# Attention between two expert layers on one core: weighted sums turned by VectorE in 32x32 blocks, quotients on GpSimd, a new order of jobs

## The chip, the cores and the metric

One Trainium2 chip, one of its cores. The metric is the device time of one execution in microseconds; the numbers before are the median of three executions.

## The reference, cut to what matters

```
x = L0_attn_x                                   # (32, 256, 128): 32 sequences of 256 tokens
x = x + 0.5 * ffn(layernorm(x))                 # 8 routed experts (top 2) + a shared one, swiglu
x = x + attn(layernorm(x))
x = x + 0.5 * ffn(layernorm(x))

def attn(x):                                    # 16 heads of 8 features
    Q, K, V = x @ W_Q.T, x @ W_K.T, x @ W_V.T
    s = where(causal, Q @ K.T / sqrt(8), -inf)
    return (softmax(s) @ V) @ W_O.T
```

The change is in `attn`; the two expert layers are computed as before.

## The kernel before, in words

The kernel runs three stages one behind the other: expert layer, attention (`attention_phase`, line 800), expert layer. x stays in SBUF throughout. Tokens are worked on in 16 chunks of 512, so a chunk of the attention is two sequences (b = 0 and 1).

**Units.** Each sequence has four units (j = 0 to 3) of four heads, so a chunk is eight units, called u0 to u7 here (u = 4b + j). A head has 32 rows in the packed tables `q_pack` and `k_pack`: three places of 8 rows with high and low halves of q and k in float16, so that one product gives the float32 accuracy, and at row 24 a place for the row's maximum. A unit uses the 32 rows of its own j in four groups.

The scores are computed twice. First as queries x keys (`scores`, line 999), only to find each row's maximum: three thirds, each a PSUM bank of 128x512 with the causal mask laid in by a product (L983) and the heads' products on top (L993); VectorE reduces each (`maxima`, L1167). This runs five units ahead. The two score banks are used in turn, so a third waits for the reduction two thirds back (line 977). The jobs m turn the negated maxima into a row of `q_pack`. Then, in the unit itself, the scores come as keys x queries with the maximum already subtracted (`scores_t`, L1025), again three thirds, each with a bank of its own; ScalarE takes the exponents into `probs` (L1241) and GpSimd sets what lies beyond the diagonal to zero (two `affine_select`, L1282). `weigh` (L1065) multiplies by V one unit later. V's table `v_ones` has a column of ones for each head, so the sum of the weights comes out with the weighted sum; the four groups write to four 32-row strips of `o_bank`, and ScalarE copies them to `o_t` (L1247).

**Jobs.** Everything else is a job, run between the units in the order of the list `PLACES` (line 761), and each job writes one of two PSUM banks in turn: a job cannot begin before the one two places ahead has been taken. x: four transposes of the normalised rows. q, k: three products of 128x512 each. Q and K (four each in a chunk, named by sequence and half): the rows of q or k are put into their places of the packed tables by two products with a 0/1 table (L926). v: twelve products. m: see above. o (four in a chunk): four transposes of `o_t` (L940), so that VectorE can take reciprocals (L1144) and multiply (L1146). y (two): two transposes of the quotients back (L949), split by ScalarE (L1231) and VectorE (L1152). z (two): the product with W_O, and VectorE adds it to x (L1155).

**Order.** Each engine runs its own list by hand. TensorE in a unit (`turn`, line 1070): thirds 0 and 1 of the unit's keys x queries product and of the scores five units ahead, interleaved so that neighbours use different rows of the array (`both`, line 1038), then third 2 of the first kind; then the first place's jobs; `weigh` of the unit before; third 2 of the scores ahead; and the jobs of the other two places. VectorE: two reductions, jobs, the third reduction, jobs; the layer norm of the chunk two ahead in u5, its scaling (L110) in u6. ScalarE: three exponents, jobs, the copy of `o_bank`. GpSimd: two masks a unit, and in u5 the inverse root of the norm (L94, an `ALU.pow` over 128x4).

To split q, ScalarE and VectorE write "stacks": a tile with the high halves of 64 rows and the low halves of the same rows, so each takes two instructions of 64 rows (L1215, L1129). Half of the Q jobs are taken by VectorE (L1134), half by ScalarE (L1219).

Of the kernel before, what the change touches and what calls it, by code (L numbers as in the profile page):

```python
# [5 lines left out]
ALU = mybir.AluOpType  # L6
# [19 lines left out]
MAX_ROW = 3 * HEAD  # L26
SCALE = float(HEAD) ** -0.5
# [34 lines left out]
LN_STEPS = 2 * TILES  # L62

# [162 lines left out]
def ffn_phase(nc, x, consts, w, norms, phase, x_dram, out, gates_dram, prepare=None):  # L226

    with ExitStack() as ctx:  # L228
# [267 lines left out]
        def _(pe):  # L496
# [91 lines left out]
            def keep_busy(n):  # L588

                pe.wait_ge(x_added, CHUNKS - 1)  # L590
                for _ in range(n):
                    nc.tensor.matmul(y_bank[CHUNKS % 2][:, :], w["w1_hi"][:, 0, :], xt_hi[turned(CHUNKS - 1)][:, :],
                                     start=True, stop=True)
# [137 lines left out]
SELECT_PARTS = 2 * 2 * ROWS // HEAD  # L731
# [3 lines left out]
def select_heads(nc, consts, done, part):  # L735

    ident = consts["ident"][:, :].rearrange("p (g j d) -> p g j d", g=GROUPS, j=UNITS)
    half = GROUPS // 2
    name, low_place = (("sel_q", 2), ("sel_k", 1))[part // (SELECT_PARTS // 2)]
    place, first = part // 2 % (ROWS // HEAD), part % 2 * half  # L740
    table = consts[name][:, :, :].rearrange("p g (j r) -> p g j r", r=ROWS)
    dst = table[:, first:first + half, :, place * HEAD:(place + 1) * HEAD]
    if place == MAX_ROW // HEAD:
        nc.vector.tensor_scalar(dst, ident[:, first:first + half, :, :], 0.0, None, ALU.mult).then_inc(done, 1)
    else:
        src = half - first if place == low_place else first
        nc.vector.tensor_copy(dst, ident[:, src:src + half, :, :]).then_inc(done, 1)


def select_max_row(nc, consts, done):  # L750
# [45 lines left out]
WARM = {"Q00": 7, "K00": 3, "Q01": 1, "first": 4}  # L796
# [3 lines left out]
def attention_phase(nc, x, consts, w, norms):  # L800

    with ExitStack() as ctx:
# [6 lines left out]
        def sem(name):  # L809
# [11 lines left out]
        stack = {m: [sb(f"{m}_stack{half}", [P, CHUNK], F16) for half in range(2)] for m in "qk"}  # L821
        half_rows = (slice(0, P // 2), slice(P // 2, P))
# [19 lines left out]
        xhi_done, qkhi_done, yhi_done, inv_done = (sem(n) for n in ("xhi_done", "qkhi_done", "yhi_done", "inv_done"))  # L842
        mask_begun = sem("mask_begun")
        scored, max_done = sem("scored"), sem("max_done")
        st_done, exp_done, masked, pv_done, o_done = (
            sem(n) for n in ("st_done", "exp_done", "masked", "pv_done", "o_done"))
# [35 lines left out]
        def _(pe):  # L882
# [14 lines left out]
            def keep_busy(n):  # L897

                for _ in range(n):
                    nc.tensor.matmul(o_bank[:, :], w_hi[:, 0, :], xt_hi[:, :], start=True, stop=True)  # L900

            def job(c, slot, name):
# [15 lines left out]
                elif kind in "QK":  # L918
# [15 lines left out]
                elif kind == "o":  # L934

                    b, t = int(name[1]), int(name[2])
                    pe.wait_ge(o_done, c * 2 * UNITS + (b + 1) * UNITS)
                    dst, done = begin(c, name)
                    for j in range(UNITS):
                        last = nc.tensor.transpose(dst[:, j * P:(j + 1) * P], o_t[b][:, j, t * P:(t + 1) * P],  # L940
                                                   ident[:, :])
                elif kind == "y":
                    b = int(name[1])

                    wait_taken(pe, c, f"o{b}0")
                    wait_taken(pe, c, f"o{b}1")
                    dst, done = begin(c, name)
                    for t in range(2):
                        last = nc.tensor.transpose(dst[:, t * P:(t + 1) * P], y[:, t, :], ident[:, :])  # L949
                elif kind == "z":  # L950

                    wait_taken(pe, c, "y" + name[1])
# [16 lines left out]
            def begin_scores(c, b, j, i):  # L969

                if j == 0 and i == 0:

                    wait_taken(pe, c, f"Q{b}1")
                    wait_taken(pe, c, f"K{b}1")
# [401 lines left out]
```

## Time and profile before

| | us |
|---|---|
| median of three runs (lowest, highest) | 1211.31 (1208.91, 1214.98) |
| the profiled execution, its own time | 1214.04 |
| its span | 1212.3 |
| first expert layer | 0 to 330.4 |
| attention | 330.4 to 899.8 |
| second expert layer | 899.8 to 1212.3 |

Over the whole span TensorE is busy for 93%, VectorE 83%, ScalarE 65% and GpSimd 47%. "Busy" counts an instruction from its start to its modelled end, and neighbouring products overlap, so for TensorE the start-to-start distances say more than the busy share. Granted clock 1.00 is the higher of two levels (2.4 GHz), 0.5 the lower. PEld is the loading of weights, which runs ahead of the products.

### The profile page before, as it was taken

The numbers are of one execution on the slowest core, as the hardware profiler recorded it, in microseconds if no ns is written. First come the engines' busy times: TensorE is split into PE (matmuls) and PEld (weight loads), VectorE is DVE, ScalarE is ACT, GpSimd is POOL, SyncE is SP. The second block draws the span as 40 slices with busy tenths as digits, with TensorE's granted clock in tenths as the row PEclk, the third lists the DMA queues.
The fourth block names the chain that finished last, engine by engine and source line by source line (L and its number), as shares of the span: only waits on it lengthen the run. The fifth ranks groups of instructions, "written<-read, shape, count | busy, mean of one in ns | idle before, by whom it ended". The sixth has DMA issues, their size and how long they took to land. (4 is left out here: it accounts for less than half of the span.)

```text
span 1212.3 us, 32050 instructions
## 1 busy us (share of the span) xinstructions
PE 1124.4 (93%) x11615; PEld 691.2 (57%) x11615; DVE 1002.0 (83%) x2583; ACT 789.4 (65%) x1545; POOL 567.7 (47%) x728
## 2 busy tenths in 40 slices
PE   3899999999989999999899999999978999999998
PEld 1566666666635555555555555555545666666665
DVE  4889999999657877888888788888758898998985
ACT  4676766767536665676676667676646667667664
POOL 2566666666603322333333223333325666666655
PEclk9899999999969998999999899999988999999999
DMA  4442443432200000000000000000004434435443
GB/s 125 153 159 90 149 144 101 136 129 85 70 1 2 2 2 1 2 2 2 2 2 2 2 2 2 2 1 2 2 2 141 145 101 151 126 114 158 117 122 97
DMA packets 59866, 80.13 MB, mean 66 GB/s; under 512 B 5568, under 2 KB 26944, under 8 KB 59712
## 3 DMA queue, kind: packets, MB, share of 16 engines
q1 hardware_dynamic: 59712, 78.08, 20.8%
q8 instruction: 96, 1.57, 0.5%
q14 instruction: 58, 0.48, 0.1%
HBM read 73.34 MB, written 4.72 MB: 64 GB/s over the span
## 5 line engine op out<-in xcount | busy, mean ns | idle before, releaser
L709 POOL TENSOR_TENSOR h_lo<-h,h_hi 128x512 f16<-128x512 f32 x288 | 333.5, 1158 | 233.9 <-ACT h_hi L656 231.8
L1167 DVE TENSOR_REDUCE neg_max_at<-score_at 128x2 f16<-128x512 f32 (+1 forms) x384 | 254.1, 691 | 80.1 <-PE score_at L993 74.9
L1282 POOL TENSOR_SCALAR_AFFINE_SELECT probs_at<-probs_at 128x512 f32<-128x512 f32 x256 | 156.3, 634 | 343.6 <-ACT probs_at L1241 343.6
L1241 ACT ACTIVATE probs_at<-prob_at 128x512 f32<-128x512 f32 x384 | 201.7, 599 | 77.3 <-PE prob_at L1025 75.2
L648 ACT ACTIVATE a<-a 128x512 f32<-128x512 f32 x256 | 149.0, 582 | 132.6 <-PE a L549 127.6
L435 DVE TENSOR_TENSOR prod<-a,gate_wide 128x512 f32<-128x512 f32 x256 | 176.0, 687 | 40.9 <-ACT a L648 40.1
L565 PE MATMUL y_b<-w_hi,h_hi 128*128 128x128 f16 x1152 | 207.8, 219 | 1.3 <-POOL h_lo L709 1.3
L565 PE MATMUL y_b<-w_lo,h_hi 128*128 128x128 f16 x1152 | 207.8, 219 | 0.0
L565 PE MATMUL y_b<-w_hi,h_lo 128*128 128x128 f16 x1152 | 207.8, 219 | 0.0
L656 ACT ACTIVATE h_hi<-h 128x512 f16<-128x512 f32 x288 | 179.5, 623 | 16.1 <-DVE h L445 15.5
L445 DVE TENSOR_TENSOR h<-prod,b 128x512 f32<-128x512 f32 x256 | 174.3, 681 | 4.9
L983 PE MATMUL score_at<-causal,ident_b 128*128 128x256 bf16 (+1 forms) x384 | 110.5, 325 | 32.0 <-ACT q_pack_at L1219 15.2
L993 PE MATMUL score_at<-k_pack_at,q_pack_at 32*128 32x128 f16 (+1 forms) x1024 | 134.4, 251 | 0.0
L565 PEld LDWEIGHTS y_b<-w_hi,h_hi 128*128 128x128 f16 x1152 | 112.7, 98 | 28.5 <-issue 1.6
L565 PEld LDWEIGHTS y_b<-w_lo,h_hi 128*128 128x128 f16 x1152 | 112.7, 98 | 27.1
L1065 PE MATMUL o_at<-probs_at,v_ones_at 128*32 128x256 f32 (+1 forms) x2048 | 116.2, 347 | 1.7 <-POOL probs_at L1282 1.7
L565 PEld LDWEIGHTS y_b<-w_hi,h_lo 128*128 128x128 f16 x1152 | 112.7, 98 | 0.0
L549 PE MATMUL a<-xt_hi,w_hi 128*128 128x512 f16 x288 | 110.6, 384 | 0.4 <-DVE prod L435 0.4
L549 PE MATMUL a<-xt_hi,w_lo 128*128 128x512 f16 x288 | 110.6, 384 | 0.0
L549 PE MATMUL a<-xt_lo,w_hi 128*128 128x512 f16 x288 | 110.3, 383 | 0.0
L549 PE MATMUL b<-xt_hi,w_hi 128*128 128x512 f16 x288 | 110.2, 383 | 0.0
L549 PE MATMUL b<-xt_hi,w_lo 128*128 128x512 f16 x288 | 110.2, 383 | 0.0
(143 smaller groups left out, 1988.3 us busy)
## 6 DMA issues: line engine op xcount, KB each, us to landing
gate_wide<-gate_rows SPq DMA_DIRECT2D x256, 256.0 KB, 5.4
x<-in_L_attn_x_dram SPq DMA_DIRECT2D x16, 256.0 KB, 6.0
out_dram<-x SPq DMA_DIRECT2D x16, 256.0 KB, 6.9
raw_w<-in_L_ffn_w_dram SPq DMA_DIRECT2D x3, 512.0 KB, 5.3
gate_rows<-gate_rows SPq DMA_DIRECT2D x32, 16.0 KB, 1.4
raw_w<-in_L_ffn_sw_dram SPq DMA_DIRECT2D x3, 64.0 KB, 3.9
raw_attn<-in_L_attn_W_Q_dram SPq DMA_DIRECT2D x1, 64.0 KB, 4.8
raw_attn<-in_L_attn_W_K_dram SPq DMA_DIRECT2D x1, 64.0 KB, 3.0
```

The costliest lines, as they stand in the source:

```text
L435: nc.vector.tensor_tensor(prod[k][:, :], a_bank[k][:, :], gate_wide[c % 2][:, e - 1, :], ALU.mult).then_inc(prod_done, 1)
L445: nc.vector.tensor_tensor(h[e % 3][:, :], prod[k][:, :], b_bank[k][:, :], ALU.mult).then_inc(h_done, 1)
L549: last = nc.tensor.matmul(dst[k][:, :], ws[:, e, :], xs[s][:, :], start=(i == 0), stop=(i == 2))
L565: last = nc.tensor.matmul(y[:, tile], hs[k][:, tile], ws[:, e, :], start=(e == 0 and t == 0 and i == 0), stop=(e == STEPS - 1 and t == TIL ...
L648: nc.scalar.activation(dst[:, :], a_bank[k][:, :], ACT.Silu).then_inc(silu_done, 1)
L656: nc.scalar.activation(h_hi[k][:, :], h[k][:, :], ACT.Copy).then_inc(hhi_done, 1)
L709: nc.gpsimd.tensor_tensor(h_lo[k][:, :], h[k][:, :], h_hi[k][:, :], ALU.subtract).then_inc(hlo_done, 1)
L993: last = nc.tensor.matmul(view[:, h, :], q_pack[slot][rows, groups[h], q0:q0 + P], k_pack[slot][rows, groups[h], first:first + keys], star ...
L1065: last = nc.tensor.matmul(o_bank[g * ROWS:(g + 1) * ROWS, t * P:SEQ], v_ones[slot][:, 2 * b + t, GROUPS * g + j, :], src, start=(t == 0), ...
L1167: nc.vector.tensor_reduce(dst, src, AX.X, ALU.max, negate=True).then_inc(max_done, 1)
L1241: nc.scalar.activation(probs[j % 2][:, i, :], prob_bank[i][:, :], ACT.Exp, scale=SCALE).then_inc(exp_done, 1)
L1282: nc.gpsimd.affine_select(out=p, in_=p, compare_op=ALU.is_ge, fill=0.0, base=0, pattern=[[0, GROUPS], [1, P]], channel_multiplier=-1).then ...
```

## The change

Six edits, all in the attention stage but for a table set up in the first expert layer.

- **o and y.** The jobs o and y are gone, and ScalarE's copy of `o_bank` with them. Two heads now share a 32-row strip (`OUT_ROWS` = 16 rows each), and all four units of a sequence stay in the one bank. At the start of the next sequence VectorE turns the bank in 32x32 blocks (`divide`, step 0, 128x512 float32), GpSimd takes the quotients (`quotient`: `pow` with -1 over 128x32, then a product over 128x256), VectorE turns them back one unit later (step 1, 128x256), ScalarE takes the high half (`split_y`), GpSimd the low (`low_y`).
- **q and k** are split as whole 128x512 tiles: one instruction of each engine per tile. A Q or K job now has four products (high table with high half, low with low) where it had two. All Q jobs are ScalarE's.
- **Banks.** Three score banks, one for each third, so that a third waits for the reduction three back; two banks for the keys x queries product, thirds 0 and 2 in one, so third 0 waits for the exponents of the unit before, and third 2 for those of third 0.
- **Third 2** of the keys x queries product is moved behind `weigh` and interleaved with third 2 of the scores (`thirds`), and ScalarE's third exponent behind the first place's jobs.
- **Norm.** Statistics and roots in u1, with a shift computed by GpSimd; the scaling is ScalarE's, in u2 and u3, two tiles each.
- **Jobs** are laid out anew in `PLACES`, 18 where there were 24, q two chunks ahead. The products that only keep TensorE busy before the stage read weights in place of the normalised x.

```diff
+OUT_ROWS = ROWS // 2
...
-PLACES = (((), ("q",), ("k",)), (("o10",), ("o11",), ("Q00",)), (("K00",), ("Q01",), ("K01",)),
-          (("m10", "m11"), ("y1",), ()),
-          (("z1",), ("Q10",), ("K10",)), (("o00",), ("o01",), ("Q11",)), (("K11",), ("y0",), ("v",)),
-          (("m00", "m01"), ("x",), ("z0",)))
+PLACES = (((), ("k",), ("Q00",)), ((), (), ("K10", "K00")), (("K01", "Q01"), ("Q10",), ()),
+          (("m10", "m11"), ("v", "z1"), ()), ((), ("K11",), ()), ((), ("x", "Q11"), ()),
+          ((), (), ("z0",)), (("m00", "m01"), (), ("q",)))
 JOBS = [name for unit in PLACES for place in unit for name in place]
-SHIFT = {n: -2 if n == "x" else -1 if n in ("m00", "m01") or n[0] in "qkQKv" else 1 if n in ("o10", "o11", "y1", "z1")
-         else 0 for n in JOBS}
-BESIDE_FIRST = [JOBS.index(n) for n in ("m10", "o00", "y0", "m00", "m00")]
+SHIFT = {n: -2 if n in "xq" else -1 if n in ("m00", "m01") or n[0] in "qkQKv" else 1 if n == "z1" else 0 for n in JOBS}
+BESIDE_FIRST = [JOBS.index(n) for n in ("Q10", "m11", "z1", "Q11", "m00")]
...
-WARM = {"Q00": 7, "K00": 3, "Q01": 1, "first": 4}
+WARM = {"q-": 5, "Q00": 2, "K10": 2, "first": 3}
...
-        stack = {m: [sb(f"{m}_stack{half}", [P, CHUNK], F16) for half in range(2)] for m in "qk"}
-        half_rows = (slice(0, P // 2), slice(P // 2, P))
+        split = {m: [sb(f"{m}_{part}", [P, CHUNK], F16) for part in ("hi", "lo")] for m in "qk"}
...
-        o_t = [sb(f"o_t{s}", [P, UNITS, SEQ], F32) for s in range(2)]
-        inv = sb("inv", [P, 2, UNITS, GROUPS], F32)
-        y = sb("y", [P, 2, P], F32)
+        o_rows = sb("o_rows", [P, 2 * SEQ // ROWS, 2, OUT_ROWS], F32)
+        inv, minus = (sb(n, [P, 2 * SEQ // ROWS, 2], F32) for n in ("inv", "minus"))
+        y = sb("y", [P, 2, SEQ // ROWS, OUT_ROWS], F32)
+        yt = sb("yt", [P, SEQ], F32)
         yt_hi, yt_lo = sb("yt_hi", [P, SEQ], F16), sb("yt_lo", [P, SEQ], F16)
-        score_bank = [bank(f"score{s}") for s in range(2)]
-        prob_bank = [bank(f"prob{i}") for i in range(3)]
+        score_bank = [bank(f"score{i}") for i in range(3)]
+        prob_bank = [bank(f"prob{s}") for s in range(2)]
...
+        def v_places(slot):
+            return v_ones[slot][:, :, :, :].rearrange("p t (n i) (k r) -> p (t n) (i k) r", i=2, r=OUT_ROWS)
+        def last_weighed(do, c, b, j):
+            if j == 0 and b == 1:
+                do(c, 0)
+            elif j == 0 and exists(c - 1):
+                do(c - 1, 1)
...
-                        last = nc.tensor.matmul(tile, consts["sel_" + m][:, 2 * half + i, :],
-                                                stack[m][half][:, tokens], start=True, stop=True)
+                        for n, part in enumerate(("hi", "lo")):
+                            last = nc.tensor.matmul(tile, consts[f"sel_{m}_{part}"][:, 2 * half + i, :],
+                                                    split[m][n][:, tokens], start=(n == 0), stop=(n == 1))
...
+                    for pack in ("Q", "K"):
+                        wait_taken(pe, c, f"{pack}{b}0")
+                        wait_taken(pe, c, f"{pack}{b}1")
                 n = c * 24 + b * 12 + 3 * j + i
-                wait_count(pe, max_done, n - 1)
-                dst = score_bank[(3 * j + i) % 2]
+                wait_count(pe, max_done, n - 2)
+                dst = score_bank[i]
...
-                wait_count(pe, exp_done, unit * 3 - 2 + i)
+                wait_count(pe, exp_done, unit * 3 + (0, -1, 1)[i])
...
-                scores_t(c, slot, b, j, parts=(2,))
+            def thirds(c, slot, b, j, ahead):
+                later, later_slot, later_b, later_j = ahead
+                part = begin_scores(later, later_b, later_j, 2)
+                begin_t(c, b, j, 2)
+                for h in range(GROUPS):
+                    head_t(slot, b, j, 2, h)
+                    if h % 2 == 1:
+                        score_head(later_slot, later_b, later_j, 2, part, h // 2)
...
-                wait_count(pe, o_done, unit)
+                if j == 0:
+                    wait_count(pe, o_step, (2 * c + b - 1) * O_STEPS + 1)
...
+                        pair = slice(j // 2 * SEQ + t * P, (j // 2 + 1) * SEQ)
+                        last = nc.tensor.matmul(o_bank[g * ROWS:(g + 1) * ROWS, pair],
                                                 v_ones[slot][:, 2 * b + t, GROUPS * g + j, :], src,
-                                                start=(t == 0), stop=(t == 1), skip_group_check=True)
+                                                start=(t == 0 and j % 2 == 0), stop=(t == 1 and j % 2 == 1),
+                                                skip_group_check=True)
...
-                            scores(*ahead, parts=(2,))
+                            thirds(c, slot, b, j, ahead)
...
+            def divide(c, b, step):
+                n = 2 * c + b
+                if step == 0:
+                    dve.wait_ge(pv_done, (n + 1) * UNITS)
+                    wait_count(dve, divided, n)
+                    done = nc.vector.transpose(o_rows[:, :, :, :].rearrange("p n i r -> p (n i r)"), o_bank[:, :])
+                else:
+                    dve.wait_ge(divided, n + 1)
+                    wait_count(dve, ylo_done, n)
+                    done = nc.vector.transpose(yt[:, :], y[:, :, :, :].rearrange("p s n r -> p n s r"))
+                done.then_inc(o_step, 1)
...
+                        last_weighed(lambda *seq: divide(*seq, 0), c, b, j)
                         if ahead:
                             maxima(ahead[0], *ahead[2:], parts=(2,))
+                        last_weighed(lambda *seq: divide(*seq, 1), c, b, j - 1)
                         turn_jobs(job, c, slot, places[1])
-                        if b == 1 and j == 1:
+                        if (b, j) == (0, 1):
...
+            def split_y(c, b):
+                act.wait_ge(o_step, (2 * c + b + 1) * O_STEPS)
+                if b == 1:
+                    wait_taken(act, c, "z0")
+                elif not is_first(c):
+                    wait_taken(act, c - 1, "z1")
+                nc.scalar.activation(yt_hi[:, :], yt[:, :], ACT.Copy).then_inc(yhi_done, 1)
+            def exponents(c, b, j, parts):
                 unit = c * 2 * UNITS + b * UNITS + j
-                for i in range(3):
+                for i in parts:
...
-                        exponents(c, b, j)
+                        exponents(c, b, j, (0, 1))
                         places = PLACES[b * UNITS + j]
                         turn_jobs(job, c, slot, places[0])
-                        if j > 0:
-                            take_o(c, b, j - 1)
-                        elif b == 1:
-                            take_o(c, 0, UNITS - 1)
-                        elif exists(c - 1):
-                            take_o(c - 1, 1, UNITS - 1)
+                        exponents(c, b, j, (2,))
                         turn_jobs(job, c, slot, places[1])
                         turn_jobs(job, c, slot, places[2])
+                        last_weighed(split_y, c, b, j - 1)
+                        if (b, j) == (0, 2):
+                            scale(c + 2, range(2))
+                        if (b, j) == (0, 3):
+                            scale(c + 2, range(2, TILES))
...
+            def quotient(c, b):
+                n = 2 * c + b
+                pool.wait_ge(o_step, n * O_STEPS + 1)
+                nc.gpsimd.tensor_tensor(inv[:, :, :], o_rows[:, :, :, HEAD], minus[:, :, :], ALU.pow).then_inc(inverted, 1)
+                pool.wait_ge(inverted, n + 1)
+                nc.gpsimd.tensor_tensor(y[:, :, :, :].rearrange("p s n (i d) -> p (s n) i d", d=HEAD),
+                                        o_rows[:, :, :, 0:HEAD],
+                                        inv[:, :, :].unsqueeze(3).to_broadcast([P, 2 * SEQ // ROWS, 2, HEAD]),
+                                        ALU.mult).then_inc(divided, 1)
+            def low_y(c, b):
+                pool.wait_ge(yhi_done, 2 * c + b + 1)
+                nc.gpsimd.tensor_tensor(yt_lo[:, :], yt[:, :], yt_hi[:, :], ALU.subtract).then_inc(ylo_done, 1)
             def turn(c, slot):
                 for b in range(2):
                     for j in range(UNITS):
                         mask(c, b, j)
-                        if b == 1 and j == 1:
+                        last_weighed(quotient, c, b, j)
+                        last_weighed(low_y, c, b, j - 1)
+                        if (b, j) == (0, 1):
                             norm_root(pool, nc, norm0 + c + 2, buf, ln_step, ln_rooted)
+                            norm_shift(pool, nc, c, norm0 + c + 2, buf, ln_rooted, shifted)
```

## Rows read from the trace of the kernel before

**Rows 1.** Windows of the attention: us, busy us of each engine (instructions), granted clock, DMA

```profile
330.40:356.60 26.20, 23.14 (x117) 10.17 (x117) 15.30 (x23) 8.60 (x13) 4.63 (x6) 0.71 0.00 1
356.60:889.70 533.10, 488.50 (x5702) 282.89 (x5701) 427.85 (x926) 361.44 (x721) 172.77 (x285) 0.96 0.01 2
```

**Rows 2.** Windows: a steady chunk (u2 to u2), and one with a clock drop

```profile
572.30:605.64 33.34, 30.31 (x369) 17.74 (x366) 27.77 (x61) 23.16 (x46) 10.94 (x18) 1.00 0.01 1
...
472.30:505.60 33.30, 30.76 (x325) 17.74 (x326) 24.73 (x54) 20.36 (x41) 9.72 (x16) 0.85 0.01 2
```

**Rows 3.** Waits of TensorE in that chunk: us in total, times, longest

```profile
PE score_at L983 <- ACT q_pack_at L1219: 1.0, 1, 1.0
PE score_at L983 <- DVE neg_max_at L1167: 1.0, 2, 0.7
PE job_at L940 <- DVE q_stack_at L1129: 0.5, 1, 0.5
PE job_at L909 <- DVE q_pack_at L1139: 0.3, 1, 0.3
```

**Rows 4.** Timeline of TensorE in unit u5: start, us, instruction, count

```profile
584.78 0.28 PE L1025 MATMUL prob_at<-q_pack_at,k_pack_at 32*128 32x256 f16 x1
...
585.23 0.38 PE L1025 MATMUL prob_at<-q_pack_at,k_pack_at 32*128 32x128 f16 x4
585.54 0.66 PE L940 MATMUL job_at<-ident,o_t_at 128*128 128x128 f32 x4
586.12 0.86 PE L1065 MATMUL o_at<-probs_at,v_ones_at 128*32 128x256 f32 x16
586.91 0.28 PE L983 MATMUL score_at<-causal,ident_b 128*128 128x256 bf16 x1
587.13 0.39 PE L993 MATMUL score_at<-k_pack_at,q_pack_at 32*128 32x256 f16 x2
587.45 0.66 PE L940 MATMUL job_at<-ident,o_t_at 128*128 128x128 f32 x4
587.94 0.38 PE L926 MATMUL job_at<-q_stack_at,sel_q 128*128 128x256 f16 x2
588.16 0.49 PE L983 MATMUL score_at<-causal,ident_b 128*128 128x512 bf16 x2
588.58 0.28 PE L1025 MATMUL prob_at<-q_pack_at,k_pack_at 32*128 32x256 f16 x1
```

**Rows 5.** Lines of VectorE in that chunk: busy us, mean ns, idle before

```profile
L1167 DVE TENSOR_REDUCE neg_max_at<-score_at 128x2 f16<-128x512 f32 (+1 forms) x25 | 16.6, 691 | 4.0 <-PE score_at L993 3.6
...
L1129 DVE TENSOR_TENSOR k_stack_at<-job_at,k_stack_at 64x512 f16<-64x512 f32 x2 | 1.4, 689 | 0.0
...
L1134 DVE CAST q_pack_at<-job_at 128x512 f16<-128x512 f32 x2 | 1.4, 680 | 0.0
L1146 DVE TENSOR_TENSOR y_at<-job_at,inv_at 128x128 f32<-128x128 f32 x4 | 1.2, 291 | 0.1
L110 DVE TENSOR_SCALAR xn<-x,moments,rstd 128x128 f32<-128x128 f32 x4 | 1.1, 341 | 0.0
L1144 DVE RECIPROCAL inv_at<-job_at 128x16 f32<-128x16 f32 x4 | 1.0, 248 | 0.0
...
L1152 DVE TENSOR_TENSOR yt_lo_at<-job_at,yt_hi_at 128x256 f16<-128x256 f32 x2 | 0.8, 425 | 0.3 <-ACT yt_hi_at L1231 0.2
```

**Rows 6.** Lines of ScalarE and GpSimd in that chunk

```profile
L1241 ACT ACTIVATE probs_at<-prob_at 128x512 f32<-128x512 f32 x24 | 12.6, 598 | 4.7 <-PE prob_at L1025 4.6
...
L1282 POOL TENSOR_SCALAR_AFFINE_SELECT probs_at<-probs_at 128x512 f32<-128x512 f32 x16 | 9.8, 634 | 20.0 <-ACT probs_at L1241 20.0
L94 POOL TENSOR_TENSOR rstd<-var_eps,power 128x4 f32<-128x4 f32 x1 | 1.0, 1006 | 0.1
L92 POOL TENSOR_TENSOR var_eps<-moments,eps 128x4 f32<-128x4 f32 x1 | 0.2, 200 | 2.3 <-DVE moments L85 2.3
```

**Rows 7.** The page's groups: GpSimd's low half in the expert layers

```profile
L709 POOL TENSOR_TENSOR h_lo<-h,h_hi 128x512 f16<-128x512 f32 x288 | 333.5, 1158 | 233.9 <-ACT h_hi L656 231.8
```

More of the change, by code:

```diff
@@ L62 @@
 LN_STEPS = 2 * TILES
+O_STEPS = 2
 def chunk_rows(x, c):
@@ L728, in _ @@
                 chunk(c)
-SELECT_PARTS = 2 * 2 * ROWS // HEAD
+SELECT_PARTS = 10
 SELECT_FROM = 4
 def select_heads(nc, consts, done, part):
[L737 to L747, printed above, removed]
+    name = ("sel_q", "sel_k")[part // (SELECT_PARTS // 2)]
+    low_place = 2 if name == "sel_q" else 1
+    step = part % (SELECT_PARTS // 2)
+    if step < 2:
+        table = consts[name + ("_hi", "_lo")[step]]
+        nc.vector.memset(table[:, :, :], 0.0).then_inc(done, 1)
+        return
+    place = step - 2
+    table = consts[name + ("_lo" if place == low_place else "_hi")][:, :, :].rearrange("p g (j r) -> p (g j) r", r=ROWS)
+    ident = consts["ident"][:, :].rearrange("p (h d) -> p h d", d=HEAD)
+    nc.vector.tensor_copy(table[:, :, place * HEAD:(place + 1) * HEAD], ident).then_inc(done, 1)
 def select_max_row(nc, consts, done):
@@ L899, in keep_busy @@
                 for _ in range(n):
-                    nc.tensor.matmul(o_bank[:, :], w_hi[:, 0, :], xt_hi[:, :], start=True, stop=True)
+                    nc.tensor.matmul(o_bank[:, :], w_hi[:, 0, :], w_hi[:, :, :].rearrange("p m n -> p (m n)"),
+                                     start=True, stop=True)
             def job(c, slot, name):
@@ L933, in job @@
                                                       (xt_lo[:, tile], w_hi[:, 2, :])))
[L934 to L949, printed above, removed]
                 elif kind == "z":
-                    wait_taken(pe, c, "y" + name[1])
+                    pe.wait_ge(ylo_done, 2 * c + int(name[1]) + 1)
                     dst, done = begin(c, name)
@@ L1086, in turn @@
                         if ahead:
-                            scores(*ahead, parts=(2,))
+                            thirds(c, slot, b, j, ahead)
+                        else:
+                            scores_t(c, slot, b, j, parts=(2,))
                         turn_jobs(job, c, slot, places[1])
                         turn_jobs(job, c, slot, places[2])
+            for name in JOBS:
+                keep_busy(WARM.get(name + "-", 0))
+                turn_jobs(job, -2, 0, (name,))
             for name in JOBS[:BESIDE_FIRST[0]]:
@@ L1126, in job @@
                 elif kind in "qk":
-                    for half, rows in enumerate(half_rows):
-                        dve.wait_ge(qkhi_done, c * 4 + (1 if kind == "q" else 3) + half)
-                        last = nc.vector.tensor_tensor(stack[kind][half][half_rows[1 - half], :], src[rows, :],
-                                                       stack[kind][half][rows, :], ALU.subtract)
-                elif kind == "Q":
-                    wait_count(dve, st_done, (c - 1) * 6 * UNITS)
-                    last = nc.vector.tensor_copy(packed(q_pack[slot], name),
-                                                 src[:, :].rearrange("p (g n) -> p g n", n=SEQ))
+                    dve.wait_ge(qkhi_done, c * 2 + (1 if kind == "q" else 2))
+                    last = nc.vector.tensor_tensor(split[kind][1][:, :], src[:, :], split[kind][0][:, :], ALU.subtract)
                 elif kind == "m":
@@ L1194, in _ @@
             run_chunks(turn)
+            for step in range(O_STEPS):
+                divide(CHUNKS - 1, 1, step)
             turn_jobs(job, CHUNKS, 0, JOBS)
@@ L1200, in job @@
                 kind = name[0]
-                if kind in "moz" or (kind == "Q" and name[2] == "0"):
+                if kind in "mz":
                     return
-                if kind == "y":
-                    b = int(name[1])
-                    if b == 1:
-                        wait_taken(act, c, "z0")
-                    elif not is_first(c):
-                        wait_taken(act, c - 1, "z1")
                 src, done = take(act, c, name)
@@ L1213, in job @@
                 elif kind in "qk":
-                    for half, rows in enumerate(half_rows):
-                        nc.scalar.activation(stack[kind][half][rows, :], src[rows, :], ACT.Copy).then_inc(qkhi_done, 1)
+                    nc.scalar.activation(split[kind][0][:, :], src[:, :], ACT.Copy).then_inc(qkhi_done, 1)
                 elif kind == "Q":
@@ L1226, in job, with scale @@
                     act.wait_ge(buffers_set, ALL_SET)
-                    nc.scalar.activation(v_ones[slot][:, :, :, 0:HEAD],
-                                         src[:, :].rearrange("p (t h d) -> p t h d", t=TILES, d=HEAD),
+                    wait_count(act, pv_done, (c - 1) * 2 * UNITS)
+                    nc.scalar.activation(v_places(slot)[:, :, 0:4:3, 0:HEAD],
+                                         src[:, :].rearrange("p (n i d) -> p n i d", i=2, d=HEAD),
                                          ACT.Copy).then_inc(done, 1)
-                elif kind == "y":
-                    nc.scalar.activation(yt_hi[:, :], src[:, 0:SEQ], ACT.Copy).then_inc(yhi_done, 1)
-            def exponents(c, b, j):
+            def scale(c, tiles):
+                act.wait_ge(shifted, 2 * (c - 2) + 2)
+                wait_taken(act, c - 1, "x")
+                for t in tiles:
+                    last = nc.scalar.activation(xn[:, t, :], chunk_rows(x, c)(t), ACT.Identity,
+                                                scale=buf["rstd"][:, t:t + 1], bias=buf["shift"][:, t:t + 1])
+                if t == TILES - 1:
+                    last.then_inc(ln_done, 1)
+            def split_y(c, b):
[6 more added lines that the diff above has]
+            def exponents(c, b, j, parts):
                 unit = c * 2 * UNITS + b * UNITS + j
-                for i in range(3):
+                for i in parts:
                     act.wait_ge(st_done, unit * 3 + i + 1)
@@ L1316, in macaron_kernel @@
         }
-        for n in ("sel_q", "sel_k"):
+        for n in ("sel_q_hi", "sel_q_lo", "sel_k_hi", "sel_k_lo"):
             consts[n] = sb(n, [P, GROUPS, P], F16)
```

62 lines of the change are left out of this document (23 added, 39 removed).

## The prediction

> **What bounds the kernel now.** I read the windows of the three stages first. The change touches attention only: 26.2 us of filling and 533.1 us of units [rows 1], and 10.1 us of emptying up to its end at 899.8. Then one steady chunk: 33.34 us, VectorE busy 27.8, ScalarE 23.2, GpSimd 10.9, TensorE 30.3 by a measure that counts overlapping products as busy [rows 2]. So no engine is plainly full and the start-to-start times of TensorE have to say whether it is. In u5 [rows 4] products of the unit's thirds 0 and 1 with the scores beside them take 585.23 - 584.78 = 0.45, third 2 alone 0.31, weigh 0.79, a causal product 0.22, third 2 of the scores 0.32, the two causal products at a unit's start 0.42: 2.51 a unit, 20.1 for eight. From the same timeline an o job is 0.58 or 0.49, a Q job 0.22; all jobs of the chunk sum to about 9.3 (four o 2.2, two y 0.55, eight Q and K 2.1, the unchanged rest 4.4). That is 29.4 of 33.34 in which TensorE issues. The waits [rows 3] are 1.0 for ScalarE's Q copy, 1.0 for a score bank that VectorE has not reduced, 0.5 and 0.3 for a job bank: 2.8, and 1.1 is left in gaps too small to be named. TensorE bounds the stage, at 88% of issue, and a third of what is lost is VectorE's lateness. VectorE itself stands idle 3.6 us a chunk for scores [rows 5]: the two wait for each other in turn.
>
> Chunks with a clock drop show 0.85 granted, that is part of the stretch at 1.2 GHz [rows 2]; the stage as a whole has 0.96 [rows 1]. 533.1 is 16 times 33.3 although the last chunk has fewer scores to do, so the drops cost some 10 to 15 us in all. I keep them as they are.
>
> **Work removed from and added to TensorE, per chunk.**
> - Four o jobs gone: 0.58 + 0.49 + twice about 0.56 = -2.2 [rows 4].
> - Two y jobs gone, two transposes each where an o has four: -0.55.
> - Eight Q and K jobs have two products of 256 columns more. The Q job's two products took 0.22 together [rows 4], so 0.11 each at the most: 16 x 0.107 (256 columns at 2.4 GHz) = +1.7.
> - `thirds`: third 2 (0.31) and the scores' third 2 (0.32) were apart. Interleaved they use different rows of the array, as thirds 0 and 1 do, where 2048 columns went by in 0.45, which is half of what they need one behind the other at 2.4 GHz. 512 beside 512 columns then take about 0.32: -0.3 x 8 = -2.4. Bounds: nothing saved, and 0.41 saved (0.63 less the 0.22 of 512 columns). I take -0.3, by the row of the interleaved thirds.
> - `weigh` has the same products in other columns: 0, and the causal and score products are as many.
> Sum -3.45: TensorE issues 26.0 us a chunk.
>
> **The other engines.** VectorE loses two of its four splits of q and k (-1.4), the casts of Q (-1.4), the product and reciprocal of o (-1.2, -1.0), the scaling (-1.1) and y's low half (-0.8): -6.9 [rows 5]. It gains two block transposes each of 128x512 from PSUM and 128x256 from SBUF. No row has one. Nearest are one-pass reads of the same shapes, 0.69 and 0.43 [rows 5], together 2.2 a chunk; upper bound four passes, about 7; lower bound 1.2, if half the time is the instruction's own. I take 2.2: VectorE 23.1, at worst 28. ScalarE loses eight copies of `o_bank` and two of four splits, gains two Q and four scalings (no dearer than an exponent, 0.60 [rows 6]): about 22. Nothing is added to SP's queue, and no DMA moves.
>
> GpSimd is where the price is open. Its masks are 16 x 0.63 [rows 6]. Added per sequence: `pow` over 128x32, a product over 128x256, the low half over 128x256. The latter two go by 1.158 for 512 columns [rows 7]: about 0.65 each. `pow` over 128x4 is 1.006 [rows 6]. An addition of the same shape is 0.20 [rows 6], so 0.8 is the power's own. If that is nearly all fixed, 32 columns cost 1.0 to 1.1; if it is all per column, 0.2 + 32 x 0.2 = 6.6. I take 2.4: the nearest row is the one of 1.0, but a quarter of the per-column bound lies on top. GpSimd then is at 10.9 + 2 x 3.7 + 0.4 for the norm's shift (two instructions like the addition) = 18.7 us a chunk, far from full. What matters is where it stands: `pow` sits ahead of the masks of the next unit.
>
> The Trainium skill (GPSIMD Engine Reference, 4.1 Engine selection) speaks against this move: elementwise work with two inputs belongs on VectorE, where it is about twice as fast. The rows agree in size (1.158 against 0.69 for 128x512). By that rule the quotients are dearer by roughly 1 us a sequence than on VectorE; by the rows that lies in idle time unless the next masks are late.
>
> **The new loops, laid out by hand with these durations.** Taking a unit's start as 0: TensorE's products 0.42 to 0.87, exponents 0 and 1 0.84 to 1.93, `weigh` to 1.66, thirds to 2.2, exponent 2 2.4 to 3.0, second mask 3.05 to 3.7. Two new conditions follow.
> - Third 0 of the next unit waits for exponent 2 (two prob banks). It is at 0.42 of the next unit, so a unit lasts at least 2.64. `weigh` waits for the mask: at least 2.9. TensorE's own 2.21 plus jobs behind `thirds` must reach that. u0, u1, u2, u3, u5 have 0.5 to 1.1 of jobs there, u4 0.5, u6 0.4, u7 0.65: about 0.2 to 0.4 in all is lost.
> - The job waits of rows 3 go: Q copies are three jobs or a unit ahead of their use, x no longer stands behind m, and q has a unit between product and Q00. The score bank waits (1.0) go too, since a third's bank is free after VectorE's reduction one whole unit back. In u3 ScalarE is late by the scaling (thirds 0 and 1 of u3 wait some 0.1) and in u4 `thirds` waits for exponent 0 about 0.3, both in the sum of lost time above.
> - `pow` starts at 3.7 after u0's masks. With p for its time, u1's masks are done at p + 5.65 and `weigh` in u1 comes at 8.26 of the chunk: free up to p = 2.6. In u5 the ready time is p + 19.55 against 20.95: free up to 1.4. With 2.4 the second costs 1.0.
>
> Next chunk starts at 26.0 + 0.35 + 1.0 + the 1.1 of small gaps, which I keep = 28.4 us. Against 33.34: -4.9 a chunk, what is late next being TensorE itself.
>
> **Sum.** 15 chunks x 4.9 = -74. The last one gains in its first three units and loses as much after, since its last five units have no scores ahead and now last 2.9 at least. Filling: one split instruction per tile in place of two, -1; emptying: four transposes fewer, `pow` and a longer chain more, 0. The table set-up in the first expert layer lies beside TensorE's products: 0. -75 against the profiled execution's 1214.0 is 1139; the runs' median lies 2.7 below that execution, so 1136.
>
> **Rivals.**
> - **`pow` is paid per column.** 6.6 us stand ahead of u1's and u5's masks; VectorE's step 1 and ScalarE's `split_y` wait behind, in order. `weigh` in u1 waits 4.1, with the norm's root behind it another 0.3, in u5 5.2. Chunk 26.35 + 9.6 = 36: slower by 2.6 x 15 = 40, 1251. It decides from p = 5.5, where the chunk is at 33.3. For: the addition's 0.20 leaves 0.8 for four columns. Against: 0.8 may be as well a set-up that is paid once. 14 in 100.
> - **The interleaving and the transposes give less.** `thirds` saves nothing (+2.4) or the transposes take four passes (VectorE 28 of 28.4, then it is the bound with its waits, about 31): chunk about 31, -35: 1176. For: `thirds` alternates after two products of the same rows. Against: the 0.45 of rows 4. 17 in 100.
> - **Everything small goes too.** `pow` fixed, the small gaps halved, and with TensorE fuller no drops: chunk 26.9, -96, and -12: 1103. 14 in 100.
> - The forecast, 1115 to 1160: 55 in 100.
>
> A rule of the Trainium skill on ports (SBUF — State Buffer, section on the two separate sides) would add a wait: VectorE and GpSimd exclude each other for a whole instruction if one of VectorE's runs in a two-port mode or has two SBUF inputs. The masks here are 634 ns on average beside a VectorE busy for 83% of the chunk; no lock is seen. By the page the SBUF transpose might meet GpSimd's product, for about 0.4 each time; that is inside the range.
>
> **How the numbers follow.** Range 1095 to 1185: it leaves out the rival on `pow` and the ends of the others. Half a per cent (6 us) is about what three runs can tell from no change here. Faster by more: all cases but `pow`, less a little for the unforeseen, 0.84; same 0.02, slower 0.14.
>
> **What would show it.** GpSimd's `pow` row over 128x32: 1 to 3 us right, above 5 the rival. TensorE's start-to-start of `thirds` 0.3 to 0.35 behind its causal product. A steady chunk of 27 to 30 us. VectorE near 23 a chunk and its transposes under 0.8. TensorE's waits for score banks gone, some for masks in u5. The prediction is wrong if TensorE waits for masks for over 3 us a chunk, or if VectorE's busy time in a chunk is within 2 us of the chunk.

## The result, and the profile after

The changed kernel takes 1278.97 us (median of four, 1278.71 to 1281.43) against 1213.14 for the kernel before (median of four, its first three runs being those of the table above): ratio 1.0544, 95% interval 1.051 to 1.0578. It is slower by 66 us; I had forecast 1136, which is faster by some 75. The profiled execution's span is 1277.1.

The attention now runs from 330.4 to 962.0, 631.6 us where it took 569.4. Windows of the changed kernel: the whole stage, and two chunks in a row (us, busy us of TensorE, weight loads, VectorE, ScalarE, GpSimd, granted clock, DMA).

```profile
330.40:962.00 631.60, 508.51 (x5798) 286.33 (x5798) 376.85 (x735) 355.47 (x673) 402.25 (x424) 0.84 0.01 1
541.34:581.01 39.67, 33.02 (x364) 18.57 (x362) 23.64 (x47) 22.19 (x43) 24.88 (x28) 0.78 0.01 2
581.01:618.34 37.33, 30.46 (x364) 17.32 (x362) 23.46 (x47) 21.98 (x43) 24.87 (x28) 0.86 0.01 1
```

Against [rows 2] VectorE has 23.5 us of work a chunk where it had 27.8, and GpSimd 24.9 where it had 10.9; none is full. The granted clock is 0.84 over the stage where it was 0.96 in the units of the kernel before [rows 1]. Four lengths of a chunk follow each other over and over, 39.7, 37.3, 35.9 and 37.3 us, 37.5 on average; the two windows are the first two of them. TensorE's waits in the second of these chunks are one kind only, where [rows 3] had four:

```profile
PE o_at L1072 <- POOL probs_at L1291: 6.8, 3, 4.0
```

`weigh` waits for masks. GpSimd's lines of that chunk (busy us, mean ns, idle before) say why; they answer to [rows 6]:

```profile
L1297 POOL TENSOR_TENSOR inv_at<-o_rows_at,minus_at 128x32 f32<-128x32 f32 x3 | 16.3, 5447 | 0.0
L1291 POOL TENSOR_SCALAR_AFFINE_SELECT probs_at<-probs_at 128x512 f32<-128x512 f32 x17 | 10.7, 636 | 12.5 <-ACT probs_at L1254 12.5
L1299 POOL TENSOR_TENSOR y_at<-o_rows_at,inv_at 128x256 f32<-128x256 f32 x2 | 1.2, 624 | 0.2
```

The `pow` takes 5.45 us, not 2.4 (x3 because the window begins and ends on one; a chunk has two). The timeline around u5, all engines, shows what stands behind it:

```profile
598.16 5.47 POOL L1297 TENSOR_TENSOR inv_at<-o_rows_at,minus_at 128x32 f32<-128x32 f32 x1
...
601.27 0.27 PE L1023 MATMUL prob_at<-q_pack_at,k_pack_at 32*128 32x256 f16 x1
...
603.71 0.62 POOL L1299 TENSOR_TENSOR y_at<-o_rows_at,inv_at 128x256 f32<-128x256 f32 x1
604.29 1.22 POOL L1291 TENSOR_SCALAR_AFFINE_SELECT probs_at<-probs_at 128x512 f32<-128x512 f32 x2
604.37 0.45 DVE L1157 STREAM_TRANSPOSE yt_at<-y_at 128x256 f32<-128x256 f32 x1 [3.95 <-POOL y_at L1299]
...
604.85 0.42 ACT L1244 ACTIVATE yt_hi_at<-yt_at 128x256 f16<-128x256 f32 x1 [3.48 <-DVE yt_at L1157]
605.17 1.07 ACT L1254 ACTIVATE probs_at<-prob_at 128x512 f32<-128x512 f32 x2
...
605.56 1.51 PE L1072 MATMUL o_at<-probs_at,v_ones_at 128*32 128x256 f32 x16 [4.01 <-POOL probs_at L1291]
```

The unit's masks start at 604.29, when product and `pow` are through, TensorE waits 4.01 us for them, and VectorE and ScalarE stand 3.95 and 3.48 us in their own queues for the same quotient. The last line shows a second loss: sixteen products of `weigh` take 1.51 us where they took 0.86 at [rows 4]. The granted clock fell to 1.2 GHz during the pause, TensorE came back from it at that clock, and stayed there until about 614. In the five chunks from 541 on this happened behind each of the five waits of 4.0 us, and behind three of the five waits of 2.56 us in u1, and the chunk with both is the longest.

### The profile page after: what moved, and what is told of

Same layout as the page of the kernel before. It is cut to its first block and busy times, and to the rows that moved or that the text cites. A ratio compares the mean times of both kernels' runs of the same rounds, so it can differ in the third digit from the quotient of the medians.

```text
span 1277.1 us, 31640 instructions
## 1 busy us (share of the span) xinstructions
PE 1117.0 (87%) x11548; PEld 682.2 (53%) x11548; DVE 928.4 (73%) x2353; ACT 773.2 (61%) x1481; POOL 791.3 (62%) x859
## 5 line engine op out<-in xcount | busy, mean ns | idle before, releaser
L1168 DVE TENSOR_REDUCE neg_max_at<-score_at 128x2 f16<-128x512 f32 (+1 forms) x384 | 251.3, 687 | 90.6 <-PE score_at L991 89.9
L1254 ACT ACTIVATE probs_at<-prob_at 128x512 f32<-128x512 f32 x384 | 214.8, 595 | 139.9 <-PE prob_at L1023 138.9
L1291 POOL TENSOR_SCALAR_AFFINE_SELECT probs_at<-probs_at 128x512 f32<-128x512 f32 x256 | 160.6, 636 | 219.0 <-ACT probs_at L1254 218.6
L1072 PE MATMUL o_at<-probs_at,v_ones_at 128*32 128x256 f32 (+1 forms) x2048 | 133.4, 387 | 108.4 <-POOL probs_at L1291 107.1
L1297 POOL TENSOR_TENSOR inv_at<-o_rows_at,minus_at 128x32 f32<-128x32 f32 x32 | 174.6, 5455 | 2.4 <-DVE o_rows_at L1153 2.4
L1072 PEld LDWEIGHTS o_at<-probs_at,v_ones_at 128*32 128x32 f32 x2048 | 59.9, 123 | 170.9 <-POOL probs_at L1291 126.1
L1023 PE MATMUL prob_at<-q_pack_at,k_pack_at 32*128 32x256 f16 (+1 forms) x1024 | 147.0, 271 | 3.2 <-ACT probs_at L1254 2.8
L991 PE MATMUL score_at<-k_pack_at,q_pack_at 32*128 32x128 f16 (+1 forms) x1024 | 144.9, 266 | 0.0
L567 PEld LDWEIGHTS y_b<-w_hi,h_hi 128*128 128x128 f16 x1152 | 112.8, 98 | 28.5 <-issue 1.6
L1023 PEld LDWEIGHTS prob_at<-q_pack_at,k_pack_at 32*128 32x128 f16 x1024 | 74.0, 101 | 72.0 <-issue 48.4
```

The lines of the kernel that those rows point to most:

```text
L567: last = nc.tensor.matmul(y[:, tile], hs[k][:, tile], ws[:, e, :], start=(e == 0 and t == 0 and i == 0), stop=(e == STEPS - 1 and t == TIL ...
L1023: last = nc.tensor.matmul(prob_bank[i % 2][:, h * width:(h + 1) * width], k_pack[slot][rows, groups[h], keys], q_pack[slot][rows, groups[h ...
L1072: last = nc.tensor.matmul(o_bank[g * ROWS:(g + 1) * ROWS, pair], v_ones[slot][:, 2 * b + t, GROUPS * g + j, :], src, start=(t == 0 and j % ...
L1168: nc.vector.tensor_reduce(dst, src, AX.X, ALU.max, negate=True).then_inc(max_done, 1)
L1254: nc.scalar.activation(probs[j % 2][:, i, :], prob_bank[i % 2][:, :], ACT.Exp, scale=SCALE).then_inc(exp_done, 1)
L1291: nc.gpsimd.affine_select(out=p, in_=p, compare_op=ALU.is_ge, fill=0.0, base=0, pattern=[[0, GROUPS], [1, P]], channel_multiplier=-1).then ...
```

## The experiments

Each ratio is to the kernel before as it ran in the same series. Its median was 1210.84 us for e1 to e4, 1206.00 for e5 to e8 and 1210.27 for e9, so that a few us between runs of different series tell nothing.

**e1: VectorE's reciprocal.**

```diff
+            def invert(c, b):
+                n = 2 * c + b
+                dve.wait_ge(o_step, n * O_STEPS + 1)
+                nc.vector.reciprocal(inv[:, :, :], o_rows[:, :, :, HEAD]).then_inc(inverted, 1)
...
                             maxima(ahead[0], *ahead[2:], parts=(2,))
+                        last_weighed(invert, c, b, j)
...
-                pool.wait_ge(o_step, n * O_STEPS + 1)
-                nc.gpsimd.tensor_tensor(inv[:, :, :], o_rows[:, :, :, HEAD], minus[:, :, :], ALU.pow).then_inc(inverted, 1)
```

> The changed kernel with one part undone: the reciprocal of the weights' sums (128x32) is VectorE's again, behind its third reduction; GpSimd keeps the product. Theory A (GpSimd's 5.46 us pow stands ahead of the next unit's masks; TensorE waits 6.8 us a chunk for them, and the pauses bring the clock down): the mask waits fall under 1 us a chunk, a chunk is 27 to 28.5 us, granted clock over the attention at least 0.95, total 1115 to 1145. Theory B (the rest of the change is no gain either: two banks for the keys x queries product, a longer chain behind o, more on GpSimd): total 1195 to 1225, with new waits of TensorE for exponents or y. A reciprocal of 32 columns costs VectorE about 0.25 us, 0.5 a chunk.

Measured: 1103.36 us, 0.9105 of before (0.9075 to 0.9136). With one instruction of 128x32 moved, the change is 9% faster than the kernel before instead of 5% slower. Theory B falls. It is also below the 1115 that theory A allowed: a chunk was to last 27 to 28.5. A chunk of this kernel (windows), and its weight loads' longest waits in it:

```profile
577.69:604.17 26.48, 26.41 (x370) 15.82 (x362) 23.63 (x49) 21.91 (x43) 14.26 (x25) 1.00 0.01 2
```

```profile
PEld prob_at L1023 <- issue: 1.6, 5, 0.3
PEld score_at L981 <- DVE neg_max_at L1173: 1.0, 5, 0.2
PEld prob_at L1023 <- ACT probs_at L1261: 1.0, 3, 0.3
```

26.48 us, full clock, no wait of TensorE itself above 0.2: the steady chunks are TensorE's from end to end. All of them last 26.5 but one of 26.8.

**e2 and e3: a shorter pow.** It runs over 8 and over 16 of the 32 columns; the other inverses stay at 1, so these two leave out three quarters and half of the inverses, with all other work unchanged.

```diff
-                nc.gpsimd.tensor_tensor(inv[:, :, :], o_rows[:, :, :, HEAD], minus[:, :, :], ALU.pow).then_inc(inverted, 1)
+                nc.gpsimd.tensor_tensor(inv[:, 0:4, :], o_rows[:, 0:4, :, HEAD], minus[:, 0:4, :], ALU.pow).then_inc(inverted, 1)
```

> The changed kernel with pow over 128x8 in place of 128x32; the other 24 inverses are left at 1, so the quotients are wrong for most rows and the rest of the work is unchanged. From 1.006 us for 4 columns and 5.457 for 32: 0.16 a column and 0.37 fixed, so 1.64 us here. Theory A: free in u1 (up to 2.6), 0.2 us late in u5: total within 15 us of the kernel with VectorE's reciprocal. If pow is stepwise in columns rather than linear: 1.0 or over 2.5 us. Theory B: as slow as before or slower, whatever pow takes.

> The same with pow over 128x16 (the other 16 inverses left at 1): 2.9 us if linear. Theory A with my hand layout: late by 0.3 in u1 and 1.5 in u5, 1.6 us a chunk more than with 8 columns, +25 us, and the clock still high as no pause passes 2 us. If the clock falls already here, +45 us or more. Theory B: no difference from 8 columns.

Measured: 1109.57 us (0.9151, 0.9114 to 0.9189) and 1148.33 (0.948, 0.9432 to 0.9527). The instructions of the two (ns, least, median, greatest):

```profile
L1297 POOL TENSOR_TENSOR inv_at<-o_rows_at,minus_at x32: 1633/1653/1675, 375.6 to 790.8; 128x8 f32<-128x8 f32 x32
```

```profile
L1297 POOL TENSOR_TENSOR inv_at<-o_rows_at,minus_at x32: 2902/2922/2941, 375.5 to 822.0; 128x16 f32<-128x16 f32 x32
```

With 1.006 for 4 columns and 5.457 for 32 the four points lie within 0.02 us of 0.37 + 0.159 a column. Chunks, from the windows:

```profile
553.89:580.65 26.76, 26.47 (x370) 15.81 (x362) 23.33 (x47) 21.91 (x43) 17.31 (x26) 1.00 0.01 3
```

```profile
568.80:597.29 28.49, 26.69 (x367) 15.77 (x363) 23.27 (x47) 21.96 (x43) 19.80 (x27) 1.00 0.01 3
```

0.28 over e1, and 1.73 more: the 0.2 and 1.6 of the layout. The total rose by 39 for the second step where 1.73 x 16 is 28, and the expectation had 25, or 45 and more if the clock fell. The runs of e3 spread from 1143.37 to 1153.75. In the profiled one, 33 us longer than that of e2, the clock fell in two chunks, which last 29.9 each, though no wait of TensorE there passes 1.5 us, and the last chunk takes 32.0 against 29.0; the rest stays open.

**e4: pow alone, in the kernel before.** Nothing reads its result.

```diff
                         mask(c, b, j)
+                        if j == 0:
+                            nc.gpsimd.tensor_tensor(spare_inv[:, :], ones[:, :], minus[:, :], ALU.pow)
```

> The kernel before with one part of the change alone: GpSimd runs a pow over 128x32 behind the masks of u0 and u4, which nothing reads. Theory A: its masks in u1 and u5 come late there too. By the trace of before: u1's masks end at 606.4 instead of 604.9 and are needed at 606.8 (nothing lost), u5's end at 590.7 and were needed at 589.7 (1.1 lost): +15 to +25 us, total 1225 to 1240. Rival C (GpSimd's instruction slows VectorE by sharing its port with it): VectorE's reductions, 691 ns, get longer beside the pow. Rival B: nothing is lost at all, under 1217, since the kernel before has units of 4.2 us.

Measured: 1224.46 us, ratio 1.0109 (1.0072 to 1.0146), 13.6 more than before and so just under the 15 to 25 that A gave. A new wait of TensorE stands among the four of [rows 3], here over 400 us, 12 chunks:

```profile
PE o_at L1066 <- POOL probs_at L1283: 11.8, 12, 1.2
```

One a chunk of 1.0 us, in u5 alone, as reckoned (1.1). VectorE's reductions last 689 ns (median; 690 in the kernel before): the `pow` does not slow them (rival C). The same instruction costs TensorE 1 us a chunk where units last 4.2 us, and in the changed kernel, whose units last 3.3 without it (e1), 6.8.

**e5: the pauses filled.** Does the clock cost time, or only show the pauses?

```diff
+                        if j == 1:
+                            name = ("K10", "x")[b]
+                            if has_job(name, c - SHIFT[name]):
+                                bank, _ = begin(c - SHIFT[name], name)
+                                for _ in range((9, 15)[b]):
+                                    nc.tensor.matmul(bank[:, :], w_hi[:, 0, :], w_hi[:, :, :].rearrange("p m n -> p (m n)"),
+                                                     start=True, stop=True)
                         if j > 0:
                             weigh(c, slot, b, j - 1)
```

> The changed kernel with its pow, but TensorE fills most of its two waits for the late masks: 9 products of 128x512 ahead of weigh in u1 (about 1.9 us of 2.6) and 15 in u5 (3.2 us of 4.0), into a job bank that is free then; nothing reads them. The waits themselves stay. Theory A in two parts: 6.8 us of waits a chunk, and some 4 to 5 us more because the clock falls to 1.2 GHz behind them. Then here a chunk is about 33.5 us, granted clock over the attention at least 0.95, total 1200 to 1225. If the late masks are all of it and the clock only shows it, total 1270 to 1285. If the fillers delay weigh, the waits for masks vanish and the total rises.

Measured: 1224.05 us (ratio 1.0136, 1.0066 to 1.0206). Useless products make the changed kernel 55 us faster (49 by the two ratios). Its chunk (windows), and the waits left in it:

```profile
570.34:603.92 33.58, 32.07 (x391) 17.95 (x387) 23.28 (x47) 21.97 (x43) 24.91 (x27) 1.00 0.01 1
```

```profile
PE o_at L1072 <- POOL probs_at L1298: 1.3, 3, 0.8
```

Its steady chunks all last 33.6, at full clock, where the changed kernel's last 37.5 on average. So of the 176 us between the changed kernel and e1, about 55 are the clock's, and 121 stay with the pauses filled: 33.58 - 26.48 = 7.1 in each steady chunk, 8.8 in the last (37.6 against 28.8), and the rest at the two ends of the stage, not looked into.

**e6 and e7: two terms of the sum, each undone on top of e1.** First the third 2 of both kinds one behind the other again, then the wait of two score banks in place of three.

```diff
-                part = begin_scores(later, later_b, later_j, 2)
-                begin_t(c, b, j, 2)
-                for h in range(GROUPS):
-                    head_t(slot, b, j, 2, h)
-                    if h % 2 == 1:
-                        score_head(later_slot, later_b, later_j, 2, part, h // 2)
+                scores_t(c, slot, b, j, parts=(2,))
+                scores(*ahead, parts=(2,))
```

```diff
-                wait_count(pe, max_done, n - 2)
+                wait_count(pe, max_done, n - 1)
```

> VectorE's reciprocal as in e1_dve_recip, and third 2 of the keys x queries product and third 2 of the scores one behind the other again (still behind weigh, same banks). The prediction's term: interleaving saves 0.3 us a unit, 2.4 a chunk: +30 to +38 us over e1_dve_recip if TensorE bounds the stage, 1133 to 1141. Rival: TensorE has slack there, 1103 to 1110.

> VectorE's reciprocal, and each third of the scores waits for the reduction two back, as with two score banks, in place of three back. The prediction's term: 1.0 us a chunk of score bank waits is gone by the third bank: +10 to +18 us over e1_dve_recip, and waits for neg_max in TensorE's list. Rival: VectorE is early enough now that its load is 5 us a chunk lower, and the third bank is worth nothing: within 3 us.

Measured: 1140.20 us and 1131.08 against e1's 1103.36 (0.9437 and 0.937 of before, where e1 has 0.9105). Windows of a chunk of e6, then of e7 with its wait:

```profile
569.24:598.06 28.82, 28.82 (x370) 16.67 (x362) 23.84 (x49) 21.97 (x43) 14.26 (x24) 1.00 0.01 3
```

```profile
562.80:590.83 28.03, 27.22 (x370) 15.89 (x362) 23.88 (x49) 21.97 (x43) 14.32 (x25) 1.00 0.01 3
```

```profile
PEld score_at L981 <- DVE neg_max_at L1173: 4.3, 13, 0.7
```

Interleaving is worth 2.34 a chunk (2.4 forecast). The third bank is worth 1.55, more than the 1.0 that TensorE's own waits showed, and 28 us in all where 10 to 18 were expected. The weight loads wait 4.3 for reductions here and 1.0 in e1: part of what I had put down as small gaps, and kept, was this.

**e8: product on VectorE too.**

```diff
-                nc.gpsimd.tensor_tensor(y[...], o_rows[..., 0:HEAD], inv[...], ALU.mult).then_inc(divided, 1)
+                nc.vector.tensor_tensor(y[...], o_rows[..., 0:HEAD], inv[...], ALU.mult).then_inc(divided, 1)
```

> Reciprocal and product both on VectorE, GpSimd keeps masks, y's low half and the norm. VectorE +0.45 us twice a chunk, less 0.63 for GpSimd ahead of u1's and u5's masks. By the layout TensorE bounds a chunk of 26.5 and neither is late: within 4 us of e1_dve_recip. If masks or y are still late there, up to 10 us faster; if VectorE is the next bound, 10 to 15 us slower.

Measured: 1103.07 us (0.9136, 0.9083 to 0.9189), the same as e1 within the noise, chunk 26.51. Quotients wholly on VectorE cost nothing here, and on GpSimd the product costs nothing: only `pow` did.

One thing shows here alone. VectorE's product has both inputs in SBUF, and where it and a mask of GpSimd overlap for 0.2 us or more, three times in the run, the later of the two takes longer. The plainest place, near the end of the stage (timeline, VectorE and GpSimd):

```profile
769.38 0.42 DVE L1165 TENSOR_TENSOR y_at<-o_rows_at,inv_at 128x256 f32<-128x256 f32 x1
769.50 0.79 POOL L1303 TENSOR_SCALAR_AFFINE_SELECT probs_at<-probs_at 128x512 f32<-128x512 f32 x1 [1.27 <-ACT probs_at L1266]
```

That mask takes 0.79 us where the others take 0.64; the two products begun under a mask take 0.54 and 0.48 us where the others take 0.43. In the steady chunks the overlap is 0.14 us at most, and nothing gets longer.

**e9: pow in four pieces.** All 32 columns stay on GpSimd, one piece of 8 behind the masks of each unit; the rest of the chain comes later.

```diff
-                pool.wait_ge(o_step, n * O_STEPS + 1)
-                nc.gpsimd.tensor_tensor(inv[:, :, :], o_rows[:, :, :, HEAD], minus[:, :, :], ALU.pow).then_inc(inverted, 1)
...
+                four = slice(4 * piece, 4 * piece + 4)
+                nc.gpsimd.tensor_tensor(inv[:, four, :], o_rows[:, four, :, HEAD], minus[:, four, :],
+                                        ALU.pow).then_inc(inverted, 1)
+                if piece < 3:
+                    return
```

> The changed kernel with all of its pow on GpSimd still, but in four pieces of 128x8, one behind the masks of each unit of the following sequence; product, turning back, halves and z come three units later (z0 and z1 change places). GpSimd's load rises: 4 x 1.65 for 5.46, twice a chunk, so about 27.5 us a chunk against 24.9. Theory A (what costs is the place of one long instruction ahead of masks that are due): TensorE's waits fall from 6.8 to under 2.5 us a chunk, chunk 28 to 30 us with GpSimd now the bound, clock over the attention at least 0.95, total 1130 to 1165. If GpSimd's load or anything else in the chain is what costs: no better than the changed kernel, 1260 or more.

Measured: 1125.80 us (0.9303, 0.9256 to 0.935), 153 us faster than the changed kernel and 4 below what A allowed, with more work on GpSimd:

```profile
584.01:611.46 27.45, 26.55 (x365) 15.85 (x366) 23.25 (x46) 21.96 (x43) 26.63 (x33) 1.00 0.01 2
```

GpSimd is busy 26.63 of 27.45 us and is now the bound, yet the masks come in time but for 12.0 us in 380. Load was not the fault; one long instruction ahead of due work was. One thing e1 and e9 do not separate: both also end the 4 us in which VectorE and ScalarE stand in their queues for the quotient. In the steady chunk of the changed kernel TensorE waits for masks alone, so that wait shows no price of its own, but no run removes it by itself. e1 and e8 stay the fastest.

## Why the prediction was wrong

**The step that failed: "I take 2.4" for `pow`.** It is 5.46, near the per-column end of my bounds (6.6). I placed the value nearest to the only row, the one of four columns, although that row could not tell a fixed cost from one per column, and although an addition of the same shape beside it left 0.8 of 1.0 to the power itself. Between two ends that decide the sign, the row chosen as nearest carried no evidence. The rest of the sum would have borne the forecast: e2, at 1.65 us, took 1110, and 0.75 us more in each of 16 chunks gives an estimate of about 1122 for 2.4 us, inside the 1115 to 1160 of the forecast.

**The layout held.** It gave p - 2.6 of waiting in u1 and p - 1.4 in u5: with p = 5.46, that is 2.9 and 4.1. The waits in u1 and u5 are 2.56 and 4.01. It gave 26.35 us for a chunk without any; e1 has 26.48. The rival on `pow` named the place, the engines that stand behind it and the point of no gain (5.5); with the real p it gives 33.3 us, even with before, and e5 has 33.58. That it fits so well is partly luck: this rival left off the 1.1 of small gaps that the forecast kept, without saying why, and they did go.

**Missing from every case: the clock.** That waits of 4 us, and some of 2.6, bring TensorE to 1.2 GHz was in none of the rivals: the sum put it at nothing. It is about 55 us, most of the way from "no change" to 5% slower; e5, without it, is still 1.4% slower than before. The low clock in the filling and in one of the two windows of the kernel before [rows 1, 2] stood in front of me, and I used it only as a constant.

**The other terms.** The transposes are 0.706 and 0.445 us (0.69 and 0.43 taken); VectorE's load a chunk is 23.5 (23.1 forecast). Q and K jobs with four products start 0.43 us apart, as reckoned. Interleaving 2.34 for 2.4. The 1.1 us of small gaps that I kept went too: with the `pow` out, "everything small goes too", which I priced at 1103 and 14 in 100, is the case of e1 (1103.36). The figure itself agrees by luck: it was made of a chunk of 26.9, and e1's is 26.48. The rule of the Trainium skill that I weighed (GPSIMD Engine Reference, 4.1 Engine selection: two-input elementwise work about twice as slow on GpSimd) has the product's direction right, though here it is 0.62 us against VectorE's 0.43 (e8), one and a half times, and hidden. A power is not of that price: 5.46 us against 0.33 for VectorE's reciprocal (e1), for an eighth of the product's columns.

The wait at a shared port that the Trainium skill describes (SBUF — State Buffer, section on the two separate sides) shows in no row of the changed kernel: its masks take 634 to 645 ns, and none of VectorE's instructions in a chunk has two SBUF inputs. In e8, where the product has them, the trace agrees with that rule, at a price of 0.05 to 0.15 us in three places. My own case for it could not arise, since the transpose in SBUF waits for GpSimd's product.

## What to carry to other kernels

An instruction on an idle engine is free only if it is short against the time until that engine's next due work: read its length and its place in the queue, not the engine's load (e9 against the changed kernel: more load, 153 us less). If the profile has one width of an unusual operation, its cost per column is unknown; where the ends of that give opposite signs, the forecast has to be split between them. And a TensorE wait of some microseconds can cost twice, once for itself and once for the slower products behind it; look for the granted clock behind the waits before adding them up.

## What the runs showed of the hardware

- GpSimd's `pow`: 1.006, 1.653, 2.922 and 5.457 us for 4, 8, 16 and 32 float32 columns of 128 partitions. VectorE's reciprocal of 128x32 took 0.330.
- VectorE's block transpose of float32: 0.706 us for 128x512 from PSUM, 0.445 for 128x256 in SBUF, close to the 0.69 and 0.43 of its other one-pass reads of these widths [rows 5].
- Clock: behind a wait of TensorE of 4.01 us the products ran at 1.2 GHz for about 9 us, and so behind all five such waits looked at, but behind only three of five waits of 2.56 us; 24 otherwise useless products of 128x512 a chunk, put into the waits, kept it at 2.4 GHz in the steady chunks and saved 55 us in all.
- Port: in e8 a mask of GpSimd that began 0.12 us behind VectorE's product, both of whose inputs are in SBUF, took 0.79 us instead of 0.64. Of the changed kernel's 256 masks, beside which VectorE has no such instruction, the longest took 0.645.
